# Maxima of an attention item in two parts with a turn each, one pair of maxima in every half-step

## The chip, the cores and the metric

The kernel runs on one core of one Trainium2 chip. The metric is the device time of one execution in microseconds (us), the median of several runs; lower is better. Engines are named as in the profile: PE (TensorE matmuls), PEld (its weight loads), DVE (VectorE), ACT (ScalarE), POOL (GpSimd), SP (SyncE, which issues most DMAs).

## The reference, cut to what matters

```python
x = layernorm(x + attention(x)); x = layernorm(x + ffn(x))    # x is (2, 2048, 256)

# attention: 16 heads of width 16, causal, two score matrices per head
std_logits = einsum('bhqd,bhkd->bhqk', q, k) * dh ** -0.5
geo_logits = einsum('bqhi,bkhi->bhqk', read_lines, J_write) * inc_scale  # i runs over 6
std_out = softmax(mask(std_logits)) @ v
geo_out = softmax(mask(geo_logits)) @ geo_v
combined = (1 - gate) * std_out + gate * geo_out          # gate: mean of 16 sigmoids per token
return combined @ out_w + out_b
```

## The kernel before, in words

Three stages follow one another: `project` (projections of all tokens to DRAM), `attend` (the two softmaxes) and `finish` (gate, output projection, feed-forward, the two norms). The change is in `attend`.

**Items.** `attend` works through 16 items; item `it` is one batch with two heads (a = 0, 1). A softmax over 2048 keys needs, for each query, the negated maximum of its DOT scores, so that the exponential stays in range. (The GEO maxima are only computed where `is_wide` is set; with these inputs that branch is not taken.) The maxima reach the scores as extra operand rows ("m rows") of the query operands: a score matmul adds them to the products, and ACT only takes the exponential.

**Steps and half-steps.** An item has 20 steps (`STEPS`), which cover the lower triangle in four query tiles of 512 queries (qt 0 to 3), two key blocks of 128 keys at a time; a step has one or two groups, and the change speaks of a group as a half-step. There are NPV = 36 half-steps, numbered 0 to 35 here: qt 0 is 0 to 2, qt 1 is 3 to 9, qt 2 is 10 to 20, qt 3 is 21 to 35. 28 of them are 512 queries wide and 8 are 384. In a half-step PE issues the GEO scores (L915, two matmuls side by side), the DOT scores (L921, four), and then the products with the values of a half-step of the step before (`earlier`, `times_v`, L988, f32, eight instructions). `ex` has two buffers: the scores of unit n wait until the exponential of unit n - 2 is done (L906). ACT takes one exponential per kind and half-step (L1074). POOL sets masked corners to zero (L887). DVE copies `pv` out at the end of each query tile (`take`, L1150).

**Maxima.** For the *next* item, PE computes the DOT scores once more with queries on the partitions (`max_pair`, L943): 40 pairs (`MAXT`: a query block of 128 against up to 512 keys; 28 pairs are 512 keys wide, and four each 384, 256 and 128), each pair two tiles, one per head. A tile goes into one of MX_RING = 3 PSUM banks, and DVE reduces it to a column of `mp` (L1101, or L1097 with the causal mask on the diagonal). The tile that comes three later waits for that (`mx_free`, L941). `spread` and `shares` deal the 40 pairs out over steps 0 to 16: in a step with two groups, one share goes between GEO and DOT of the first group, one between GEO and DOT of the second, and one behind DOT of the second. In step 17 (`MT_STEP`) comes `max_rows`: DVE reduces `mp` to `negm` (L1131), PE transposes it (L968), DVE splits it in two bf16 parts in `mrow` (L1139, L1141), and SP copies these to the m rows of the next item by 8 small DMAs (`rows`, L785).

**The order of SP in an item** (`item`, from L788) is written out by hand: store of the last query tile of the item before; the first six operand loads for item `it + 2` (a DMA of 128 KB each for the DOT operands); `store(it, 0)`; six more loads; in item 0 a wait for `gts_ready` and the store of the gates (L806); in item 8 the loads of the denominators of the first batch (L230, L234); `store(it, 1)`; six loads; the value operand; `store(it, 2)`; six loads; and at last `rows(it + 1)`, which waits for `mrow_ready`. PE waits for the m rows at the start of an item (`m_in`). Items 14 and 15 have no operand loads to issue.

**Prologue.** Before item 0, PE and DVE do the 40 pairs and the transposition of item 0 with nothing beside them, then DVE works out the gates (`gates_`, L1186 to L1193). The transposition of the gates is in item 0 behind step 18 (L1032), DVE copies it to `gts` (L1173), and this sets `gts_ready`, for which SP waits at L806.

**The loop.** PE's code is item 0, then a loop of four rounds of three items each (1 to 12), then items 13 to 15 written out.

Of the kernel before, what the change touches and what calls it, by code (L numbers as in the profile page):

```python
# [115 lines left out]
NMX = NTILE + 1  # L116
MX_RING = 3
MT_STEP = NSTEP - 3
# [3 lines left out]
def spread():  # L122

    room = [sum(width(s, j) for j in range(len(STEPS[s][1]))) + P if s < MT_STEP else 0 for s in range(NSTEP)]
    cost = [w + (220 if d else 150) for _, _, w, d in MAXT]
    out, u, done = [], 0, 0
    for i in range(NSTEP):
        mine = []
        while u < NMT and done + cost[u] / 2 <= sum(cost) * sum(room[:i + 1]) / sum(room):
            mine.append(u)  # L130
            done += cost[u]
            u += 1
        out.append(mine)
    assert u == NMT
    return out


MAX_IN = spread()


def shares(s):

    n, places = len(MAX_IN[s]), 1 + len(STEPS[s][1])
    out, at = [], 0
    for i in range(places):
        m = (n + places - 1 - i) // places
        out.append(MAX_IN[s][at:at + m])
        at += m
    return out
# [557 lines left out]
def attend(nc, parts, values, raw, gates, ident, mask_qk, gate_z, wide, out_w, out_b, wg, wu, wd, weights,  # L707
           sets, fixed, rden, x, late):
    with ExitStack() as ctx:
# [12 lines left out]
        mp = [sb(f"mp{i}", [P, 2 * NKB, NQT]) for i in range(2)]  # L722
        dull = sb("dull", [P, MX_RING, CH])
        negm = sb("negm", [P, P])
        mrow = sb("mrow", [4 * NKB, 2, P], BF16)
# [7 lines left out]
        m_in = sem("m_in")  # L733
# [8 lines left out]
        wx_ready = sem("wx_ready")  # L742
        wx_free = sem("wx_free")
        wx_rows = sem("wx_rows")
        negm_ready = sem("negm_ready")
        mrow_high = sem("mrow_high")
        mrow_ready = sem("mrow_ready")
# [15 lines left out]
        def _(q):  # L763
# [11 lines left out]
            def rows(it, to):  # L775

                q.wait_ge(mrow_ready, it + 1)
                q.sem_inc(passed, 1)
                for a in range(2):
                    for i in range(2):  # L780
                        geo = to["geo"][0][HALF * a + GEO_ROWS + i:HALF * a + GEO_ROWS + i + 1, :]
                        dot = to["dot"][0][HALF * a + DOT_MINOR + i:HALF * a + DOT_MINOR + i + 1, 1, :]
                        for kind, dst in ((GEO, geo), (DOT, dot)):
                            n = (2 * kind + a) * NKB
                            q.dma_start(dst.rearrange("p (k t) -> p k t", t=P),  # L785
                                        mrow[n:n + NKB, i, :]).then_inc(m_in, 16)

            def item(it):  # L788
# [40 lines left out]
                if it + 1 < ITEMS:  # L829
                    rows(it + 1, sets[(it + 1) % NSET])  # L830
# [3 lines left out]
            rows(0, sets[0])  # L834
# [9 lines left out]
        def _(g):  # L844

            g.memset(negm[:, :], 0.0).then_inc(cleared, 1)
            for i in range(2):
                g.wait_ge(cleared, i + 1)
                g.memset(mp[i][:, :, :], MASKED).then_inc(cleared, 1)
            g.wait_ge(cleared, 3)  # L850
# [48 lines left out]
        def _(pe):  # L899
# [26 lines left out]
            def max_pair(nxt, u):  # L926

                nit, which, use = nxt
                q_set, k_set = sets[which]["dot"]
                first = isinstance(nit, int) and nit == 0  # L930
                if u == 0:

                    pe.wait_ge(sets[which]["dot_in"], (use + 1) * LOADS * 16)
                    if not first:
                        pe.wait_ge(mrow_ready, nit)
                qb, k0, w, _ = MAXT[u]
                for a in range(2):
                    t = 2 * u + a
                    if t >= MX_RING:

                        pe.wait_ge(mx_free, nit * NTILE + t + 1 - MX_RING)  # L941
                    rows = slice(HALF * a, HALF * a + DOT_MAIN)
                    pe.matmul(mx[:, t % MX_RING, 0:w], q_set[rows, 0, qb * P:(qb + 1) * P],  # L943
                              k_set[rows, 0, k0:k0 + w], start=True, stop=True).then_inc(mx_ready, 1)

            def wide_pair(nxt, u):
                nit, which, use = nxt
                q_set, k_set = sets[which]["geo"]
                if u == 0:
                    pe.wait_ge(mx_free, nit * NTILE + NTILE)  # L950
                    pe.wait_ge(sets[which]["geo_in"], (use + 1) * LOADS * 16)
                else:

                    pe.wait_ge(wx_free, nit * NMT + u)
# [5 lines left out]
                last.then_inc(wx_ready, 1)  # L960

            def max_rows(nxt):
                with pe.If(is_wide > 0):
                    for u in range(NMT):
                        wide_pair(nxt, u)

                pe.wait_ge(negm_ready, nxt[0] + 1)
                pe.transpose(mx[:, (NMX - 1) % MX_RING, 0:P], negm[:, :], ident[:, :]).then_inc(mx_ready, 1)  # L968

            def times_v(it, which, use, s, j, head):  # L970
# [10 lines left out]
                if s == FIRST_OF[qt] and j == 0 and not (head and qt == 0):  # L981

                    pe.wait_ge(on_ready, it * NQT + qt)
# [11 lines left out]
            def step(at, before, nxt, s, head):  # L995

                it, which, use = at
                places = shares(s) if nxt else [[] for _ in range(1 + len(STEPS[s][1]))]
                groups = len(STEPS[s][1])

                def some(i):
                    for u in places[i]:
                        max_pair(nxt, u)
# [18 lines left out]
            def item(at, before, nxt, head):  # L1022
# [11 lines left out]
                if head:  # L1034

                    pe.wait_ge(gts_ready, 1)
# [4 lines left out]
            def prologue():  # L1041
                for u in range(NMT):
                    max_pair(static(0), u)
                max_rows(static(0))
# [39 lines left out]
        def _(v):  # L1084
            v.wait_ge(cleared, 3)
            is_wide = v.value_load(wide[0:1, 0:1], min_val=0, max_val=1)

            def max_pair(nit, u):
                qb, k0, w, on_diagonal = MAXT[u]
                for a in range(2):  # L1090
                    t = 2 * u + a
                    to = mp[DOT][:, a * NKB + qb, k0 // CH:k0 // CH + 1]

                    v.wait_ge(mx_ready, nit * NMX + t + 1)
                    if on_diagonal:
                        v.sem_inc(v_passed, 1)
                        last = v.tensor_tensor_reduce(  # L1097
                            out=dull[:, t % MX_RING, 0:w], in0=mx[:, t % MX_RING, 0:w], in1=mask_qk[:, CH - w:CH],
                            scale=1.0, scalar=3 * MASKED, op0=ALU.add, op1=ALU.max, accum_out=to)
                    else:  # L1100
                        last = v.tensor_reduce(out=to, in_=mx[:, t % MX_RING, 0:w], axis=AX.X, op=ALU.max)  # L1101
                    last.then_inc(mx_free, 1)
# [475 lines left out]
```

## Time and profile before

| | |
|---|---|
| median of 3 runs | 1913.83 us (1912.52 to 1914.31) |
| the profiled execution's own time | 1911.92 us |
| its span, first to last instruction | 1910.2 us |
| mean granted TensorE clock | 0.944 |
| PE busy | 1686.7 us (88%) |
| ACT busy | 1218.8 us (64%) |
| DVE busy | 1057.9 us (55%) |
| POOL busy | 336.5 us (18%) |
| idle of ACT before an exponential, ended by PE's GEO scores | 256.0 us |

The stage `project` runs to about 229 us of the span, `attend` to about 1568 us, `finish` to the end. A profile's groups give, for each line, engine and form, the busy time, the mean duration and the idle time of the engine just ahead of it with what ended it. The timeline gives the start and the length of runs of equal instructions in order; the length of a run of matmuls reaches from its first start to its last (modelled) end.

### The profile page before, as it was taken

Reading aid. Unit: us, or ns where it says so; the run is one execution under the profiler, and the core shown is the slowest. Engines: PE = TensorE matmul, PEld = TensorE weight load, DVE = VectorE, ACT = ScalarE, POOL = GpSimd, SP = SyncE. Lnnn points to the kernel's source line nnn. Section 1 sums busy time; section 2 is a strip of 40 time slices with the busy share of each in tenths; the row PEclk is TensorE's granted clock in tenths of the full one; section 3 lists DMA queues with packets and bytes.
Section 4 is the critical chain, followed back from the end, with each engine's and each line's share of the span. In section 5 each row is a group of like instructions: output and inputs, shape, how many; then the busy total and the mean of one; then the engine's idle time right before and its main releaser. Section 6 shows DMA issues by size and latency. Waiting matters only on the chain. (4 is left out here: it accounts for less than half of the span.)

```text
span 1910.2 us, 36280 instructions
## 1 busy us (share of the span) xinstructions
PE 1686.7 (88%) x11793; PEld 606.2 (32%) x11793; DVE 1057.9 (55%) x2509; ACT 1218.8 (64%) x1457; POOL 336.5 (18%) x478
## 2 busy tenths in 40 slices
PE   7887469679999999999989999999999874999998
PEld 4544112122222222222222222222222222565555
DVE  4775586355755657556565565755756103545432
ACT  3553308568888788887878878888888861211221
POOL 4432402012111111111111111111110213112000
PEclk9998659889999999999999999999999987999999
DMA  5774511112211111111120111111102004232000
GB/s 170 215 216 145 164 62 41 63 45 77 87 44 67 44 61 73 42 61 57 51 86 34 67 45 59 73 42 62 71 33 68 18 25 152 72 101 97 11 22 22
DMA packets 97400, 140.67 MB, mean 74 GB/s; under 512 B 8144, under 2 KB 66320, under 8 KB 95152
## 3 DMA queue, kind: packets, MB, share of 16 engines
q1 hardware_dynamic: 96000, 135.08, 20.6%
q0 software_dynamic: 624, 2.75, 0.4%
q8 instruction: 111, 1.82, 0.4%
q14 instruction: 89, 0.73, 0.1%
q10 hardware_dynamic: 576, 0.28, 0.1%
HBM read 81.96 MB, written 55.61 MB: 72 GB/s over the span
## 5 line engine op out<-in xcount | busy, mean ns | idle before, releaser
L1074 ACT ACTIVATE prob<-ex 128x1024 f32<-128x1024 f32 (+1 forms) x1152 | 1050.2, 978 | 276.9 <-PE ex L915 256.0
L1101 DVE TENSOR_REDUCE mp<-mx 128x1 f32<-128x512 f32 x768 | 487.9, 685 | 170.2 <-PE mx L943 170.2
L988 PE MATMUL pv<-prob,va 128*32 128x512 f32 (+3 forms) x5120 | 581.1, 545 | 0.6 <-POOL prob L887 0.6
L887 POOL TENSOR_SCALAR_AFFINE_SELECT prob<-prob 128x256 f32<-128x256 f32 (+1 forms) x384 | 186.1, 485 | 1124.1 <-ACT prob L1074 1119.9
L1097 DVE CUSTOM_DVE_ANT_0 dull<-mx,mask_qk 128x128 f32<-128x128 f32 (+3 forms) x512 | 231.5, 487 | 258.1 <-PE mx L943 256.5
L921 PE MATMUL ex<-dq,dk 34*128 34x512 bf16 (+7 forms) x2560 | 344.5, 352 | 29.3 <-ACT prob L1074 28.6
L943 PE MATMUL mx<-dk,dq 64*128 64x512 bf16 (+3 forms) x1280 | 305.0, 363 | 40.4 <-DVE mp L1101 20.5
L915 PE MATMUL ex<-gq,gk 38*128 38x512 bf16 (+3 forms) x1280 | 221.4, 358 | 46.0 <-DMA dq<-mrow 34.4
L915 PEld LDWEIGHTS ex<-gq,gk 38*128 38x128 bf16 x1280 | 57.3, 93 | 440.4 <-ACT prob L1074 368.5
L988 PEld LDWEIGHTS pv<-prob,va 128*32 128x32 f32 x5120 | 115.2, 109 | 227.9 <-issue 191.4
L1427 ACT ACTIVATE sg<-pg 128x512 f32<-128x512 f32 x48 | 28.7, 597 | 246.0 <-PE pg L1367 243.1
L921 PEld LDWEIGHTS ex<-dq,dk 64*128 64x128 bf16 (+1 forms) x2560 | 99.4, 95 | 175.3 <-ACT prob L1074 131.2
L943 PEld LDWEIGHTS mx<-dk,dq 64*128 64x128 bf16 x1280 | 86.8, 96 | 159.2 <-DVE mp L1101 90.5
L1150 DVE COPY on<-pv 128x512 f32<-128x512 f32 x64 | 44.3, 692 | 99.6 <-PE pv L988 98.8
L470 POOL TENSOR_TENSOR sp<-d,sp 128x512 bf16<-128x512 f32 (+1 forms) x48 | 68.8, 1448 | 141.0 <-ACT sp L565 141.0
L1367 PE MATMUL pg<-y_t,wg_f 128*128 128x512 f32 x192 | 90.8, 595 | 1.8 <-DVE ht L1507 1.7
L1367 PE MATMUL pg<-y_t,wu_f 128*128 128x512 f32 x192 | 90.2, 592 | 0.0
L1383 PE MATMUL po<-wd_f,ht 128*128 128x256 f32 x384 | 85.0, 381 | 5.7 <-DVE ht L1507 5.7
L489 PE MATMUL pn<-wv,xc 128*128 128x512 f32 x128 | 64.4, 628 | 22.5 <-DVE vn L641 14.4
L1383 PEld LDWEIGHTS po<-wd_f,ht 128*128 128x128 f32 x384 | 72.3, 190 | 17.6 <-issue 5.1
L508 PE MATMUL pr<-xc,wqk 128*128 128x512 f32 x128 | 63.8, 656 | 14.9 <-ACT sp L559 14.9
L1507 DVE SCALAR_TENSOR_TENSOR ht<-pg,sg 128x512 f32<-128x512 f32 x48 | 33.0, 690 | 76.7 <-ACT sg L1427 76.7
(98 smaller groups left out, 886.8 us busy)
## 6 DMA issues: line engine op xcount, KB each, us to landing
values<-vn SPq DMA_DIRECT2D x32, 512.0 KB, 5.2
va<-values SPq DMA_DIRECT2D x16, 1024.0 KB, 13.3
raw<-on SPq DMA_DIRECT2D x64, 256.0 KB
parts_dot<-sp SPq DMA_DIRECT2D x32, 384.0 KB, 5.0
dq<-parts_dot SPq DMA_DIRECT2D x96, 128.0 KB
dk<-parts_dot SPq DMA_DIRECT2D x96, 128.0 KB
att<-raw SPq DMA_DIRECT2D x32, 256.0 KB
rr<-rden SPq DMA_DIRECT2D x32, 256.0 KB
```

The lines of the kernel that those rows point to most:

```text
L470: g.tensor_tensor(out=sp3[m][0:n, SLOTS[m][2], :], in0=d32[m][0:n, :], in1=sp3[m][0:n, SLOTS[m][1], :], op=ALU.subtract).then_inc(p3_done, 1)
L489: pe.matmul(bank[:, 0, :], xc[par][:, k, tok], wv[:, k, :], start=k == 0, stop=k == NK - 1)
L887: g.affine_select(out=cut, in_=cut, compare_op=ALU.is_ge, fill=0.0, base=0, pattern=[[0, nb], [1, P]], channel_multiplier=-1).then_inc(mas ...
L915: last = pe.matmul(ex[:, n % 2, a * CH + at:a * CH + at + w], k_set[rows, keys], q_set[rows, queries], start=True, stop=True)
L921: last = pe.matmul(ex[:, n % 2, a * CH + at:a * CH + at + w], k_set[rows, part, keys], q_set[rows, part, queries], start=part == 0, stop=p ...
L943: pe.matmul(mx[:, t % MX_RING, 0:w], q_set[rows, 0, qb * P:(qb + 1) * P], k_set[rows, 0, k0:k0 + w], start=True, stop=True).then_inc(mx_re ...
L988: last = pe.matmul(pv[blk * VW:(blk + 1) * VW, CH - w:CH], sets[which]["v"][:, kb, blk * VW:(blk + 1) * VW], prob[UNIT_AT[s, j, kind] % NP ...
L1074: act.activation(prob[n % NPROB][:, :].rearrange("p (b c) -> p b c", b=2)[:, :, 0:w], ex[:, n % 2, :].rearrange("p (b c) -> p b c", b=2)[: ...
L1097: last = v.tensor_tensor_reduce(out=dull[:, t % MX_RING, 0:w], in0=mx[:, t % MX_RING, 0:w], in1=mask_qk[:, CH - w:CH], scale=1.0, scalar=3 ...
L1101: last = v.tensor_reduce(out=to, in_=mx[:, t % MX_RING, 0:w], axis=AX.X, op=ALU.max)
L1367: last = pe.matmul(pg[m % 2][:, i, :], w[:, k, m * P:(m + 1) * P], y_t[:, k, :], start=k == 0, stop=k == NK - 1)
L1383: last = pe.matmul(po[tt % 2][:, 0:D], ht[:, m, tt * P:(tt + 1) * P], wdf[:, m, :], start=m == 0, stop=m == NM - 1)
```

## The change

The 40 pairs of an item are split in two parts: EARLY holds the 24 pairs of query tiles 0 to 2, LATE the 16 pairs of query tile 3. Each part has its own `negm`, `mrow`, semaphores and turn. The EARLY turn stands in half-step 30 of the item before. The LATE turn stands in half-step 9 of the item itself. Pairs stand only between the GEO and the DOT scores of a half-step. `max_places` gives these places (an entry is the keys of the pair, all in one half-step):

| half-step | pairs |
|---|---|
| 0 to 8 | LATE of this item, one pair of 512 each |
| 9 | none; LATE turn |
| 10 | EARLY of the next item: 128, 256 and 384 |
| 11 to 27 | EARLY: one pair each (512; 384 in half-steps 19 and 20) |
| 28, 29 | EARLY: 128 and 256 in each |
| 30 | none; EARLY turn |
| 31 | LATE of the next item: 128, 256 and 384 |
| 32 to 35 | LATE: one pair of 512 each |

The prologue is what stands in half-steps 10 to 35, without scores; the first 9 LATE pairs of every item are now in the item. SP's `rows` is called twice per item: for LATE behind the second six operand loads, ahead of `store(it, 1)`, with 4 rows of 128 values per DMA; for EARLY at the end as before, with 12 rows per DMA (before: 16). PE waits for the EARLY m rows at the start of an item and for the LATE ones ahead of step 12 (half-step 21). The transposition of the gates and their copy to `gts` move from item 0 to the prologue, behind the EARLY turn, and use `pv` for it.

```diff
-MAX_IN = spread()
+PARTS = ((0, 1, 2), (3,))
+EARLY, LATE = 0, 1
+TURN = (30, 9)
...
+    early = [cuts(0, 0, 1, 2), cuts(0, 3)] + fulls(1) + [cuts(1, 3)] + fulls(2)[0:2] + [cuts(1, 2), cuts(2, 2)]
+    early += fulls(2)[2:] + [cuts(2, 3), cuts(1, 0, 1), cuts(2, 0, 1)]
+    late = [cuts(3, 0, 1, 2)] + fulls(3) + [cuts(3, 3)]
...
+MAX_IN = max_places()
+LEAD = TURN[LATE] + 1
...
-            def rows(it, to):
-
-                q.wait_ge(mrow_ready, it + 1)
+            def rows(it, part, to):
+
+                q.wait_ge(mrow_ready[part], it + 1)
                 q.sem_inc(passed, 1)
+                n, first = PART_BLOCKS[part], PART_FIRST[part] * P
+                cols = slice(first, first + n * P)
...
                             q.dma_start(dst.rearrange("p (k t) -> p k t", t=P),
-                                        mrow[n:n + NKB, i, :]).then_inc(m_in, 16)
+                                        mrow[part][at:at + n, i, :]).then_inc(m_in[part], 16)
...
                     load_den(q, raw, gates, 0, late)
+                rows(it, LATE, sets[it % NSET])
                 store(it, 1)
                 load(range(12, 18))
...
-                    rows(it + 1, sets[(it + 1) % NSET])
+                    rows(it + 1, EARLY, sets[(it + 1) % NSET])
...
                 for j in range(groups):
+                    h = PV_AT[s, j]
+                    to = at if h < LEAD else nxt
                     scores(it, which, s, j, GEO, head)
-                    some(j)
+                    if to:
+                        for u in MAX_IN[h]:
+                            max_pair(it, to, u)
                     scores(it, which, s, j, DOT, head)
-                    if j == groups - 1:
-                        some(groups)
-                    if j == 0 and s == MT_STEP and nxt:
-                        max_rows(nxt)
+                    if to and h in TURN:
+                        turn(it, to, TURN.index(h))
                     earlier(j)
...
-                pe.wait_ge(m_in, (it + 1) * 128)
+                pe.wait_ge(m_in[EARLY], (it + 1) * 128)
                 for s in range(NSTEP):
+                    if s == FIRST_OF[PARTS[LATE][0]]:
+                        pe.wait_ge(m_in[LATE], (it + 1) * 128)
                     step(at, before, nxt, s, head)
-                    if head and s == NSTEP - 2:
-
-                        pe.wait_ge(gate_ready, 5)
-                        pe.transpose(mx[0:2 * NC * TT, 0, 0:P], gate[:, :, :].rearrange("p i n -> p (i n)"),
-                                     ident[:, :]).then_inc(gate_turned, 1)
...
             def prologue():
-                for u in range(NMT):
-                    max_pair(static(0), u)
-                max_rows(static(0))
+                for h in range(LEAD, NPV):
+                    for u in MAX_IN[h]:
+                        max_pair(-1, static(0), u)
+                    if h in TURN:
+                        turn(-1, static(0), TURN.index(h))
+
+                        pe.wait_ge(gate_ready, 5)
+                        pe.transpose(pv[0:2 * NC * TT, 0:P], gate[:, :, :].rearrange("p i n -> p (i n)"),
+                                     ident[:, :]).then_inc(gate_turned, 1)
```

## Rows read from the trace of the kernel before

**Rows 1.** Waits of PE, whole span: us in total, times, longest
```profile
PE ex L915 <- DMA dq<-mrow: 34.4, 2, 27.4
```
**Rows 2.** Timeline of PE, item 12, half-steps 16 and 17 (start, length)
```profile
1290.27 0.39 PE L915 MATMUL ex<-gq,gk 38*128 38x512 bf16 x2
1292.24 0.39 PE L915 MATMUL ex<-gq,gk 38*128 38x512 bf16 x2
...
1293.22 0.80 PE L943 MATMUL mx<-dk,dq 64*128 64x512 bf16 x2
...
1294.95 0.39 PE L915 MATMUL ex<-gq,gk 38*128 38x512 bf16 x2
```
**Rows 3.** Timeline of the prologue: DVE's first tile, PE's sixth
```profile
232.18 0.29 DVE L1097 CUSTOM_DVE_ANT_0 dull<-mx,mask_qk 128x128 f32<-128x128 f32 x1 [8.49 <-PE mx L943]
...
233.16 0.10 PEld L943 LDWEIGHTS mx<-dk,dq 64*128 64x128 bf16 x1 [0.27 <-DVE mp L1097]
```
**Rows 4.** Timeline of PE: the transposition of item 12
```profile
1323.68 0.33 PE L968 MATMUL mx<-ident,negm 128*128 128x128 f32 x1
```
**Rows 5.** Timeline of PE: GEO scores of half-steps 0 and 21, and next item
```profile
1256.65 0.39 PE L915 MATMUL ex<-gq,gk 38*128 38x512 bf16 x2
...
1301.35 0.39 PE L915 MATMUL ex<-gq,gk 38*128 38x512 bf16 x2
...
1333.09 0.39 PE L915 MATMUL ex<-gq,gk 38*128 38x512 bf16 x2
```
**Rows 6.** Timeline of SP, item 12: first store, last of twelve loads issued
```profile
1259.28 0.55 SPq L772 DMA_DIRECT2D raw<-on  x1
...
1281.67 4.78 SPq L225 DMA_DIRECT2D dk<-parts_dot  x3
```
**Rows 7.** The page's DMA issues: count, KB each
```profile
raw<-on SPq DMA_DIRECT2D x64, 256.0 KB
...
dq<-parts_dot SPq DMA_DIRECT2D x96, 128.0 KB
```
**Rows 8.** Windows: busy us per engine, PEclk, DMA share of 16 engines, GB/s
```profile
1260.00:1301.00 41.00, 39.49 (x356) 11.12 (x352) 29.60 (x72) 34.76 (x39) 7.26 (x15) 1.00 0.13 52
```
**Rows 9.** Timeline: the m rows of item 1 and the gate they wait behind
```profile
361.97 0.53 SPq L806 DMA_DIRECT2D gates<-gts  x1
...
383.35 0.59 SPq L785 DMA_DIRECT2D dq<-mrow  x1
...
391.24 0.61 PE L915 MATMUL ex<-gq,gk 38*128 38x512 bf16 x2 [27.37 <-DMA dq<-mrow]
```
**Rows 10.** Line L785, all m row DMAs: issue to landing
```profile
DMA to landing us min/median/max: 1.7/1.8/7.8
```
**Rows 11.** Timeline, item 8: denominators' gates issued by SP, awaited by DVE
```profile
969.38 2.51 SPq L234 DMA_DIRECT2D den_gate<-gates  x2
...
984.89 3.35 DVE L241 RECIPROCAL den<-den 128x512 f32<-128x512 f32 x1 [5.46 <-DMA den_gate<-gates]
```
**Rows 12.** Timeline of PE: transposition of the prologue, first scores of item 0
```profile
278.18 0.47 PE L968 MATMUL mx<-ident,negm 128*128 128x128 f32 x1 [3.60 <-DVE negm L1131]
...
285.73 0.61 PE L915 MATMUL ex<-gq,gk 38*128 38x512 bf16 x2 [7.07 <-DMA dq<-mrow]
```
**Rows 13.** Windows before and after the last operand load of the prologue
```profile
274.00:278.00 4.00, 0.59 (x1) 0.08 (x1) 1.90 (x6) 0.00 (x0) 0.00 (x0) 0.50 0.13 51
278.00:280.00 2.00, 0.47 (x1) 0.18 (x1) 1.36 (x5) 0.00 (x0) 0.00 (x0) 0.50 0.01 4
```
**Rows 14.** Timeline of PE: start of item 7
```profile
857.32 0.61 PE L915 MATMUL ex<-gq,gk 38*128 38x512 bf16 x2 [2.53 <-issue]
```
**Rows 15.** Windows: the same place, PEclk and the rest
```profile
857.00:868.00 11.00, 10.61 (x72) 3.82 (x72) 4.50 (x18) 5.49 (x7) 2.91 (x6) 0.53 0.08 23
```
**Rows 16.** Timeline of DVE, item 15
```profile
1494.26 2.28 DVE L1178 TENSOR_TENSOR att<-att,rr 128x2048 f32<-128x2048 f32 x1
```
**Rows 17.** Groups of DVE by form: a full tile of maxima, count, busy, mean ns
```profile
L1101 DVE TENSOR_REDUCE mp<-mx 128x1 f32<-128x512 f32 x768 | 487.9, 685 | 170.2 <-PE mx L943 170.2
```

More of the change, by code:

```diff
@@ L115 @@
 NTILE = 2 * NMT
-NMX = NTILE + 1
 MX_RING = 3
-MT_STEP = NSTEP - 3
 DEN_STEP = 10
[L122 to L134, printed above, removed]
-    return out
@@ L138 @@
-MAX_IN = spread()
[L141 to L149, printed above, removed]
+PARTS = ((0, 1, 2), (3,))
+EARLY, LATE = 0, 1
+TURN = (30, 9)
+PART_BLOCKS = [TT * len(qts) for qts in PARTS]
+PART_FIRST = [TT * qts[0] for qts in PARTS]
+PART_OF = [next(p for p in range(2) if qb // TT in PARTS[p]) for qb, _, _, _ in MAXT]
@@ new lines, with __init__, add, ready @@
+MAX_IN = max_places()
+LEAD = TURN[LATE] + 1
+class Ring:
+    def __init__(self):
+        self.order, self.bank, self.tiles, self.part = [], [], [], []
+        at, tiles = 0, 0
+        for h in range(NPV):
+            for u in MAX_IN[h]:
+                for a in range(2):
+                    self.add((u, a), at % MX_RING, tiles, None)
+                    at, tiles = at + 1, tiles + 1
+            for part in range(2):
+                if h == TURN[part]:
+                    self.add(("turn", part), at % MX_RING, None, part)
+                    at += 1 if part == EARLY else 3
+            if h == LEAD - 1:
+                self.head, self.head_tiles = len(self.order), tiles
+        assert tiles == NTILE and at % MX_RING == 0
+        self.uses = len(self.order)
+        self.place = {use: i for i, use in enumerate(self.order)}
+    def add(self, use, bank, tile, part):
+        self.order.append(use)
+        self.bank.append(bank)
+        self.tiles.append(tile)
+        self.part.append(part)
+    def ready(self, it, i):
+        return (it + 1) * self.uses - self.head + i + 1
+    def freed(self, it, i):
+        return (it + 1) * NTILE - self.head_tiles + self.tiles[i] + 1
+    def owner(self, i):
+        j = i - 1
+        while self.bank[j] != self.bank[i]:
+            j -= 1
+        return j % self.uses, j < 0
@@ L152, in set_of, with item_of @@
+RING = Ring()
+EARLY_FIRST = MAX_IN[LEAD][0]
+def item_of(it, part):
+    return it + 1 if part == EARLY else it
 def set_of(k, i):
@@ L731, in attend @@
         pv = pb("pv", [P, CH])
-        m_in = sem("m_in")
+        m_in = [sem(f"m_in{p}") for p in range(2)]
         cleared = sem("cleared")
@@ L980, in times_v @@
                     pe.wait_ge(sets[which]["v_in"], (use + 1) * 16)
-                if s == FIRST_OF[qt] and j == 0 and not (head and qt == 0):
-                    pe.wait_ge(on_ready, it * NQT + qt)
+                if s == FIRST_OF[qt] and j == 0:
+                    if head and qt == 0:
+                        pe.wait_ge(gts_ready, 1)
+                    else:
+                        pe.wait_ge(on_ready, it * NQT + qt)
                 at = 0
@@ L1089, in max_pair @@
+            def max_pair(it, u):
                 qb, k0, w, on_diagonal = MAXT[u]
                 for a in range(2):
-                    t = 2 * u + a
-                    to = mp[DOT][:, a * NKB + qb, k0 // CH:k0 // CH + 1]
-                    v.wait_ge(mx_ready, nit * NMX + t + 1)
+                    i = RING.place[u, a]
+                    v.wait_ge(mx_ready, RING.ready(it, i))
                     if on_diagonal:
                         v.sem_inc(v_passed, 1)
[L1097 to L1101, printed above, removed]
```

205 lines of the change are left out of this document (113 added, 92 removed).

## The prediction

> **What bounds the kernel now.** I read the waits of PE first, then the timelines. The largest wait of PE in `attend` is for m rows, 34.4 us in two waits [rows 1]: one before item 0, one of 27.4 us before item 1. Inside an item I compared half-steps. With one pair between GEO and DOT, the next GEO comes 1.97 us later (1290.27 to 1292.24); with a second pair behind DOT it is 2.71 us (1292.24 to 1294.95), because its tiles, 0.80 us long instead of 0.39, wait for a bank that DVE has not emptied [rows 2]. The last item, without maxima, isn't faster per half-step than with one pair: one pair hides in the wait of DOT for the exponential. So the double pairs are what a stream of one pair can save. An item in the steady middle lasts 76.44 us (1256.65 to 1333.09), of which 44.70 lie before half-step 21 (1301.35) and 31.74 behind it [rows 5].
>
> A third resource nearly fills the item: SP's DMAs. From 1260 to 1301 their share is a flat 0.13, some two of 16 engines, at 52 GB/s [rows 8]. SP has issued the last of the twelve loads by 1286.5 [rows 6], but what stands in the queue, two stores of 256 KB and twelve loads of 128 KB [rows 7], is 2.1 MB and takes 40.3 us at 52 GB/s: from 1260 to about 1300.5. The queue is 14 us behind SP.
>
> **The change, part by part.** All terms are in us of the profiled execution (1911.92).
>
> *Gates in the prologue.* Before, SP stands at the wait for `gts_ready` until 361.97, and everything behind it in SP's order is late; the last m row of item 1 is issued at 383.35 and PE starts item 1 at 391.24, after 27.37 us idle [rows 9]. With the gates ready before item 0, SP runs ahead as in other items: -27.4.
>
> *A shorter prologue.* The 9 LATE pairs of half-steps 0 to 8 leave it: 18 full tiles at 0.635 (487.9 / 768) [rows 17], 11.4. The EARLY m rows can now fly while DVE does the gates and the other LATE tiles, which ended with PE's start at 285.73 at the latest [rows 12], so at 274.3 now. But the two busy DMA engines still carry the loads of item 1: share 0.13 until 278, 0.01 after that [rows 13]. The m rows stand behind these, and land in 1.8 (median) [rows 10]: start at 279.6, so -6.1. Bounds: -11.4 and 0.
>
> *LATE m rows in the item.* They are issued behind the twelve loads, at 1286.5 on item 12's scale, and PE needs them at half-step 21. If they stood alone they would land about 7 us later (eight issues of 0.6, then 1.8), at 1293.5, in time. I hold that they don't stand alone. An m row DMA behind a full queue landed 7.8 after its issue instead of 1.8 [rows 10], and it was item 1's, PE waiting [rows 9]. In item 8 another DMA, issued just behind the same twelve loads, from 969.38, landed at 984.89, some 13 us after its issue had ended (969.38 + 2.51) [rows 11]. So the LATE m rows land when the queue has drained, 1300.5 to 1301, plus 1.8 and a little for eight small DMAs: 1303.2. PE would be ready at 1301.35 or, with what half-steps 0 to 20 save, at 1300.2: their double pairs go (0.7 each for those of two full pairs, as in rows 2, less for the short ones, 2.5 in all), six tiles in half-step 10 (1.1, priced below) and the second transposition, 0.33 [rows 4], come. So PE waits 3 us and resumes 46.5 into the item instead of 44.7: +1.8 per item. What is saved before half-step 21 is lost in this wait. Bounds: -1.1 (landed in time) and +3.
>
> The Trainium skill, "DMA: Bandwidth & Descriptors", section "Why a DMA increments its semaphore by 16 and not by 1", says that such a DMA is spread over as many engines, at most 16, as divide the slowest dimension of both sides, and takes the lowest-numbered ones. By this rule the loads (slowest dimension 2) sit on two engines, as the share of 0.13 shows, and LATE's 4 rows on four engines that include these two; no run here shows which engines a DMA of 4 rows takes. By the rule the sum stands; if it did not hold, the sum would be that of the first rival.
>
> *Half-steps 21 to 35.* Gone: the double pairs of half-steps 22, 24 and 28, scaled from the 0.74 of [rows 2] by their width: about 0.25 + 0.5 + 0.7 = 1.45. New: half-steps 28 and 29 have two cut pairs ahead of DOT, 31 has three. The prologue shows the price of six such tiles in three banks: the sixth starts 0.98 after DVE began the first [rows 3]. A tile's matmul starts 0.2 behind GEO, DVE begins 0.4 to 0.5 later, so DOT starts 1.6 behind GEO instead of 0.5: +1.1. With four tiles it is about 1.1 instead of 0.5: +0.6, twice. The LATE pairs in 32 to 35 hide as others do: +0.1 (0 to +1). The EARLY turn costs what it cost before. Together -1.45 + 1.1 + 1.2 + 0.1 = +1.0 (bounds -1 and +2.5).
>
> *Sum per item:* +2.8. It holds in items 1 to 7 and 9 to 13 (12 items). Four of them (1, 4, 7, 10) begin with a disturbed stretch that the wait now covers, so I count 1.8 there: 8 x 2.8 + 4 x 1.8 = +29.6. In item 8 PE already waits near half-step 21 for DVE and the denominators: +1. Item 14 has no loads, so no wait: -1.1 + 1.0, about 0. Item 15 now has LATE pairs, and DVE's 2.28 for `att` [rows 16] and 1.2 for the mix stand in the middle of them: +2.5. In item 0 the queue has a head start: 0.
>
> *TensorE's clock.* Before item 7 PE was idle for 2.53, and then 0.53 of full speed was granted on average over the next 11 us, that is the 1.2 GHz level for most of it [rows 14, 15]. A wait of 3 us at half-step 21 should do the same at times. In such a stretch ACT bounds two of three half-steps, so it costs less than the half: between 0 and 3, I take 1.4 in 12 items: +17.
>
> SP issues 8 more DMAs per item (5 us); before, it stood waiting about 10 us for the turn, so this is free, and the second turn costs DVE under 1 us of idle time. EARLY m rows leave one half-step sooner: no cost.
>
> **Sum:** -27.4 - 6.1 + 29.6 + 1 + 2.5 + 17 = +16.6, so 1928.5 for the profiled execution. The median of the runs shown lies 1.9 above that execution (1913.83 against 1911.92): **1930.4**.
>
> **The rivals.**
> 1. *LATE m rows land in time*, being small and on engines that are free. For it: at a share of 0.13 some 14 of 16 engines are free [rows 8], and 1.8 is the median landing [rows 10]. Against: the two rows of late landings above. Then each item is -1.1 + 1.0, about 0, nothing is idle and the clock holds: -27.4 - 6.1 + 2.5 = -31, **1883** with the 1.9. The point: landing before 44 us of the item. Chance 0.18.
> 2. *The wait is there, but the clock holds* or the wait is nearer 2 us: the 17 fall away, **1913**, within the noise of the measurement, which can't tell less than about 0.2% (4 us) from no change. Chance 0.18.
> 3. *The stream is better than I price it*: six tiles cost little since PE can place them beside DOT in other rows of the array, -1 instead of +1 behind half-step 21 takes 24 from the twelve items, and the clock drops in half of them, 8 less: 1930.4 - 32 = **1898**. Chance 0.12.
> 4. *The change doesn't do what it says*: the stream isn't even (three half-steps hold two or three pairs). That is in my sum.
>
> My forecast with its neighbours, slower, has 0.52. Slower by over 0.2%: 0.52 and a third of rival 2, 0.58. Within 0.2%: 0.13. Faster: the rest, 0.29. The forecast's own range is 1919 to 1946. The whole range is 1888 to 1947: it reaches down to rival 3 and leaves out rival 1 at 1883 and the highest costs of clock and wait, some 0.2 together.
>
> **What would show it.** PE's waits: a new one at L915 for the DMA of `mrow` of 2 to 4 us in some 12 items, and the one of 27 us gone; item 0 starting near 280; GEO of half-step 21 at 46.5 of the item, the item 79 to 81 long; waits of L943 for DVE in half-steps 10, 28, 29 and 31; a lower mean clock in `attend`. The landing of L785's DMAs would have two groups. Wrong is the forecast if PE does not wait at half-step 21.

## The result: slower, and by more than forecast

| | before | after |
|---|---|---|
| median | 1913.17 us, shared runs (1911.44 to 1914.31) | 1953.66 us of 4 runs (1952.89 to 1961.90) |
| ratio | 1 | 1.0222, 95% interval 1.0194 to 1.0251 |
| profiled execution | 1911.92 us | 1961.90 us |
| mean granted TensorE clock | 0.944 | 0.934 |

The forecast was 1930.4 (1888 to 1947). Its direction was right, its size too small by 23 us, and the time lies outside its range. The profiled execution of after is the slowest of its four, 8 us above their median. I compare profile with profile below (+50.0 us) and median with median in the experiments; so some 8 of the 50 us are this execution's own. One of the 11 executions of before beside e1 to e4 took 3938 us, and the ratios leave it out.

The page of after, busy times and one of its groups (line engine op, tiles, count, busy, mean ns, idle before):

```profile
PE 1693.0 (86%) x11809; PEld 601.8 (31%) x11809; DVE 1083.8 (55%) x2557; ACT 1230.1 (63%) x1457; POOL 337.4 (17%) x479
...
L1164 DVE TENSOR_REDUCE mp<-mx 128x1 f32<-128x512 f32 x768 | 492.3, 686 | 321.4 <-PE mx L1008 302.2
```

A full tile of maxima takes DVE 686 ns, as before [rows 17]. PE's busy time grew by 6.3 us of the 50, DVE's by 26, but DVE is busy for only 55% of the span. So PE's time went into idle stretches. Waits of PE in after (us in total, times, longest):

```profile
PE ex L973 <- DMA dq<-mrow: 40.3, 14, 9.0
...
PE mx L1008 <- DVE mp L1161: 35.3, 73, 1.7
```

The one wait of 27.4 for the gates is gone from [rows 1]. What is left are a wait before item 0 (9.0, before 7.1) and, new, one at half-step 21 of 13 items. Waits of DVE in after, those that no other engine ends ("issue"); the same view of before lists none at these two lines, only 2.1 us once at `negm` and 0.3 at a masked tile:

```profile
DVE mp L1164 <- issue: 16.2, 4, 4.1
DVE on L1221 <- issue: 4.7, 4, 1.3
```

This is the row that I had not reckoned with. Item 12, the item of [rows 2], [rows 5] and [rows 6], shows both. Timeline of PE in after: GEO of half-steps 0, 21, 28 to 32, and of the next item:

```profile
1282.96 0.39 PE L973 MATMUL ex<-gq,gk 38*128 38x512 bf16 x2
...
1333.02 0.39 PE L973 MATMUL ex<-gq,gk 38*128 38x512 bf16 x2 [3.39 <-DMA dq<-mrow]
...
1349.09 0.39 PE L973 MATMUL ex<-gq,gk 38*128 38x512 bf16 x2
...
1351.72 0.39 PE L973 MATMUL ex<-gq,gk 38*128 38x512 bf16 x2
...
1354.35 0.39 PE L973 MATMUL ex<-gq,gk 38*128 38x512 bf16 x2
...
1356.37 0.39 PE L973 MATMUL ex<-gq,gk 38*128 38x512 bf16 x2
...
1359.81 0.39 PE L973 MATMUL ex<-gq,gk 38*128 38x512 bf16 x2
...
1368.17 0.39 PE L973 MATMUL ex<-gq,gk 38*128 38x512 bf16 x2
```

The item lasts 85.21 instead of 76.44: 50.06 before half-step 21 (before: 44.70), and 35.15 behind it (31.74). Half-steps 28 and 29, with two cut pairs ahead of DOT, take 2.63 each, 31 with three takes 3.44.

DVE in after at the start of the same item, and then SP:

```profile
1281.08 1.29 DVE L1164 TENSOR_REDUCE mp<-mx 128x1 f32<-128x512 f32 x2 [0.57 <-PE mx L1008]
1286.41 1.29 DVE L1164 TENSOR_REDUCE mp<-mx 128x1 f32<-128x512 f32 x2 [4.04 <-issue]
1287.62 0.68 DVE L1221 COPY on<-pv 128x512 f32<-128x512 f32 x1
```
```profile
1288.39 0.55 SPq L827 DMA_DIRECT2D raw<-on  x1
...
1296.04 14.71 SPq L280 DMA_DIRECT2D dq<-parts_dot  x3
1310.79 4.78 SPq L280 DMA_DIRECT2D dk<-parts_dot  x3
1315.69 2.23 SPq L842 DMA_DIRECT2D gq<-mrow  x1
...
1322.14 0.57 SPq L842 DMA_DIRECT2D dq<-mrow  x1
```

DVE stands idle for 4.04 us between the last pair of one item and the first of the next, though PE's first tile of the new item, started at 1283.18, is done by 1283.6. This is where DVE's own loop (one item per round) jumps back: in the trace of after the branch stands on DVE's sequencer (which issues its instructions) at 1281.28, the first instruction of the next round (it sets registers) at 1284.07, and the one after it at 1286.41. Before, the same place lay in steps 17 to 19, which had no pairs. The branch stands at 1248.11, the next instruction at 1250.86, and DVE is idle there for 8.98 us anyway, with PE as the releaser. DVE in before:

```profile
1257.29 0.29 DVE L1097 CUSTOM_DVE_ANT_0 dull<-mx,mask_qk 128x128 f32<-128x128 f32 x1 [8.98 <-PE mx L943]
...
1258.50 0.69 DVE L1150 COPY on<-pv 128x512 f32<-128x512 f32 x1 [0.60 <-PE pv L988]
```

In after pairs stand on both sides of the jump. PE's pair must wait for a bank, DVE's copy of `pv` comes 4.7 into the item instead of 1.85, SP's first store, which waits for that copy, 5.4 instead of 2.6 [rows 6], and all of SP's order with it: the last LATE m row is issued 39.2 into the item and PE's wait for it ends at 50.06.

**Where the 50.0 us went.** Each half-step is measured from the start of its first exponential to the next; sums are after less before, in the profiled executions, beside what the prediction's terms say.

```
                                    predicted   measured
start of item 0                        -6.1        -5.9
length of item 0 (the gates)          -27.4       -26.5
items 1 to 14, half-steps 0 to 20     +17.5       +51.9
    of it half-steps 0 to 2                       +16.5
    half-steps 3 to 19                             +3.0
    half-step 20 (ends in the wait)               +32.5
items 1 to 14, half-steps 21 to 35    +30.0       +27.2
item 15                                +2.5        +3.5
sum                                   +16.5       +50.2
```

(The prediction's 17.5: 8 items of +1.8, 4 of +0.8, item 8 +1, item 14 -1.1. Its 30.0: 13 items of +1.0 and 17 for the clock.) One line is wrong, by 34.4. The others are off by up to 2.8 each, and their misses nearly cancel (0.7 together).

### The profile page after: what moved, and what is told of

Its sections match the earlier page's. It is cut to its first block and busy times, and to the rows that moved or that the text cites. A ratio compares the mean times of both kernels' runs of the same rounds, so it can differ in the third digit from the quotient of the medians.

```text
span 1960.2 us, 36600 instructions
## 1 busy us (share of the span) xinstructions
PE 1693.0 (86%) x11809; PEld 601.8 (31%) x11809; DVE 1083.8 (55%) x2557; ACT 1230.1 (63%) x1457; POOL 337.4 (17%) x479
## 3 DMA queue, kind: packets, MB, share of 16 engines
q8 instruction: 111, 1.82, 0.4%
## 5 line engine op out<-in xcount | busy, mean ns | idle before, releaser
L1145 ACT ACTIVATE prob<-ex 128x1024 f32<-128x1024 f32 (+1 forms) x1152 | 1061.5, 977 | 315.8 <-PE ex L973 234.1
L1062 PE MATMUL pv<-prob,va 128*32 128x512 f32 (+3 forms) x5120 | 594.0, 556 | 0.5 <-POOL prob L945 0.5
L979 PE MATMUL ex<-dq,dk 34*128 34x512 bf16 (+7 forms) x2560 | 356.1, 360 | 23.2 <-ACT prob L1145 19.9
L1008 PE MATMUL mx<-dk,dq 64*128 64x512 bf16 (+3 forms) x1280 | 276.0, 370 | 68.8 <-DVE mp L1161 35.3
L973 PE MATMUL ex<-gq,gk 38*128 38x512 bf16 (+3 forms) x1280 | 227.3, 367 | 65.3 <-DMA dq<-mrow 40.3
L979 PEld LDWEIGHTS ex<-dq,dk 34*128 34x128 bf16 (+1 forms) x2560 | 102.1, 97 | 182.3 <-ACT prob L1145 148.2
L1008 PEld LDWEIGHTS mx<-dk,dq 64*128 64x128 bf16 x1280 | 81.7, 96 | 134.5 <-DVE mp L1161 73.8
```

Source lines behind the costliest of these rows:

```text
L973: last = pe.matmul(ex[:, n % 2, a * CH + at:a * CH + at + w], k_set[rows, keys], q_set[rows, queries], start=True, stop=True)
L979: last = pe.matmul(ex[:, n % 2, a * CH + at:a * CH + at + w], k_set[rows, part, keys], q_set[rows, part, queries], start=part == 0, stop=p ...
L1008: pe.matmul(mx[:, RING.bank[i], 0:w], q_set[rows, 0, qb * P:(qb + 1) * P], k_set[rows, 0, k0:k0 + w], start=True, stop=True).then_inc(mx_r ...
L1062: last = pe.matmul(pv[blk * VW:(blk + 1) * VW, CH - w:CH], sets[which]["v"][:, kb, blk * VW:(blk + 1) * VW], prob[UNIT_AT[s, j, kind] % NP ...
L1145: act.activation(prob[n % NPROB][:, :].rearrange("p (b c) -> p b c", b=2)[:, :, 0:w], ex[:, n % 2, :].rearrange("p (b c) -> p b c", b=2)[: ...
```

## Experiments

**Theories.** A, the prediction's: the LATE m rows are late because their DMAs queue behind operand loads that move at 52 GB/s on few DMA engines. B: DVE's jump costs PE some 2.5 us per item by itself and delays SP's order, which adds to A's wait. C, the rival to both: the stream itself, with its bunches of pairs in half-steps 10, 28, 29 and 31, is the loss, and the waits would only move.

**e1, e2, e3: the two waits alone and together.** e1 writes DVE's items out, so that it has no loop:

```diff
-            with v.Fori(1, PAIRS_OF_HEADS) as it:
-                item(it, False, True)
-            item(PAIRS_OF_HEADS, False, True)
-            with v.Fori(PAIRS_OF_HEADS + 1, ITEMS - 1) as it:
-                item(it, False, True)
+            for it in range(1, ITEMS - 1):
+                item(it, False, True)
```

> The changed kernel with DVE's two loops over items 1 to 7 and 9 to 14 written out, nothing else. Theory A (DVE's jump back at the end of a loop round costs it about 3 to 4 us; before, it fell in steps 17 to 19, where DVE had no pairs, now pairs stand on both sides of it): the idle time of about 4 us ahead of DVE's first tile of an item is gone in items 2 to 7 and 10 to 14, half-steps 1 and 2 together take 4.2 us as in items 1, 4 and 9 instead of 7 to 8.6, and the stores of SP, with the whole DMA queue, come 2 to 3 us earlier. Part of it is taken back by a longer wait for the LATE m rows at half-step 21, so 1953.7 falls to 1932 to 1948. Rival B (DVE is late for another reason, for instance the copy of pv or the m rows): nothing moves, 1950 to 1957.

e2 issues the LATE m rows ahead of the second six loads:

```diff
                 store(it, 0)
+                rows(it, LATE, sets[it % NSET])
                 load(range(6, 12))
...
-                rows(it, LATE, sets[it % NSET])
                 store(it, 1)
```

> The changed kernel with the 8 DMAs of the LATE m rows issued ahead of the second six operand loads instead of behind them. Theory A (they land late because they stand in the rings behind twelve loads that two DMA engines work off): PE's wait for them at half-step 21 (now 2 to 4 us in 12 items) is gone, half-steps 0 to 20 take 46 to 47 us instead of 48 to 50, the clock drops less often, 1953.7 falls by 30 to 45, to 1909 to 1924. Rival B (small DMAs of 4 rows are slow by themselves, or mrow is ready late): the wait stays, 1945 to 1957.

e3 does both.

> Both edits: DVE's items written out and the LATE m rows first. Theory A for both: an item takes 43.6 + 33.1 = 76.7 us, nothing waits for m rows or for DVE's jump: 1883 to 1895, clearly under the sum of what each edit brings alone, since alone the one's gain is partly taken by the other's wait. Rival: the two gains add up or the queue finds another wait: over 1900.

Measured against the kernel before (1912.94 in these runs): e1 1940.23 (ratio 1.0147, 1.0117 to 1.0176), e2 1921.20 (1.0043, 1.0021 to 1.0065), e3 1883.28 (0.9851, 0.9821 to 0.9881). All three lie in the ranges expected. Taken from 1953.66, e1 gives back 13.4, e2 32.5, both 70.4. The two costs hide each other: with only DVE's jump gone PE is at half-step 21 earlier and waits longer there; with only the wait gone the jump's loss remains. Waits of PE in e1:

```profile
PE ex L973 <- DMA dq<-mrow: 56.2, 14, 9.1
```

e1 is the kernel that the prediction priced, the change without a cost of DVE's loop. Its half-steps 0 to 20 of items 1 to 14 are 31.4 longer than before, where the prediction's terms say 17.5, and its median is 9.8 above the forecast. So this line was priced 14 too low without any cost of DVE's loop, and the waits for the LATE m rows are why: in the twelve items besides item 8 PE waits 3.1 to 4.1 us, and half-steps 0 to 20 are 2.6 to 3.0 longer in the eight steady ones instead of 1.8; in item 8 they are 5.0 longer instead of 1. The other 20.5 of the table's 34.4 come from DVE's loop.

In e3, where only the one before item 0 is left:

```profile
PE ex L973 <- DMA dq<-mrow: 8.9, 1, 8.9
```

e3's item 12 on PE, GEO of half-steps 0 and 21 and of the next item, and DVE at its start:

```profile
1222.99 0.39 PE L973 MATMUL ex<-gq,gk 38*128 38x512 bf16 x2
...
1266.81 0.39 PE L973 MATMUL ex<-gq,gk 38*128 38x512 bf16 x2
...
1299.69 0.39 PE L973 MATMUL ex<-gq,gk 38*128 38x512 bf16 x2
```
```profile
1223.63 1.29 DVE L1164 TENSOR_REDUCE mp<-mx 128x1 f32<-128x512 f32 x2 [1.23 <-PE mx L1008]
1224.89 0.69 DVE L1221 COPY on<-pv 128x512 f32<-128x512 f32 x1
```

The item is 76.70 long, 43.82 + 32.88. The idle 4 us of DVE are gone and its copy comes 1.9 into the item, as before the change. In e3 half-steps 0 to 2 of items 1 to 14 sum to 7.9 less than before and 3 to 19 to 6.9 less; in after they were 16.5 and 3.0 more. The difference is 24.4 + 9.9 = 34.3; between e2 and e3, which differ in DVE's loop alone, it is 23.4 + 9.2 = 32.6, some 2.4 us per item. That this is near the table's miss of 34.4 is chance: with the loop's loss PE comes later to half-step 21 and waits less there, so in after the loop costs 20.5, and the rest is the wait. A and B both hold. C doesn't: without the two waits the kernel is 30 us faster than before.

**e4: how much of that is the stream?** The kernel before, with nothing but the transposition and copy of the gates moved into the prologue (for PE; DVE's copy moves the same way, and PE waits for `gts_ready` before `pv` is first used):

```diff
                     step(at, before, nxt, s, head)
-                    if head and s == NSTEP - 2:
-                        pe.wait_ge(gate_ready, 5)
-                        pe.transpose(mx[...], gate[...], ident[:, :]).then_inc(gate_turned, 1)
-                if head:
-                    pe.wait_ge(gts_ready, 1)
...
                 max_rows(static(0))
+                pe.wait_ge(gate_ready, 5)
+                pe.transpose(pv[...], gate[...], ident[:, :]).then_inc(gate_turned, 1)
```

> The kernel before with one part of the change alone: the gates are transposed and copied in the prologue. Theory: PE's wait of 27.4 us ahead of item 1 is gone and nothing else changes: 1913.2 falls to 1883 to 1887. Rival (SP is late in item 0 for its queue as well, and the wait only shrinks): 1890 to 1905.

Measured: 1880.08 (0.9844, 0.9814 to 0.9874), 32.9 below its 1912.94 and 3 below the range expected. Item 1 starts at

```profile
363.33 0.39 PE L915 MATMUL ex<-gq,gk 38*128 38x512 bf16 x2
```

on PE, instead of after the wait that ended at 391.24 [rows 9]; its steady items keep their 76.43. So e3, with the even stream, is no faster than e4 without it (1883.3 and 1880.1): the gates are the whole gain of e3, and the even stream brought 0.9 per item in half-steps 0 to 20 and lost 1.15 behind them.

**e5: the bunches.** In e3 a half-step with several pairs keeps one between GEO and DOT and puts the others behind DOT:

```diff
-                        for u in MAX_IN[h]:
+                        for u in MAX_IN[h][:1]:
                             max_pair(it, to, u)
                     scores(it, which, s, j, DOT, head)
+                    if to:
+                        for u in MAX_IN[h][1:]:
+                            max_pair(it, to, u)
```

> The kernel of e3 (DVE's items written out, LATE m rows first), and in half-steps with more than one pair only the first pair stands between GEO and DOT, the others behind DOT. Theory (the even stream's gain is eaten by half-steps 10, 28, 29 and 31, where DOT stands behind 4 or 6 tiles in 3 banks: 3.08, 2.63, 2.63 and 3.29 us in e3): they fall to about 2.3, 2.2, 2.2 and 2.6, an item of 76.7 to 74.4, 1883.3 to 1850 to 1860. Rival (DVE's time for the six tiles decides, wherever they stand): 1875 to 1886.

Measured: 1863.36, against 1908.78 of before in these runs (0.9755, 0.9739 to 0.9771), 3 above what was expected. GEO of half-steps 28 to 32 on PE:

```profile
1266.67 0.39 PE L973 MATMUL ex<-gq,gk 38*128 38x512 bf16 x2
...
1268.87 0.39 PE L973 MATMUL ex<-gq,gk 38*128 38x512 bf16 x2
...
1271.07 0.39 PE L973 MATMUL ex<-gq,gk 38*128 38x512 bf16 x2
...
1273.17 0.39 PE L973 MATMUL ex<-gq,gk 38*128 38x512 bf16 x2
...
1276.23 0.39 PE L973 MATMUL ex<-gq,gk 38*128 38x512 bf16 x2
```

28 and 29 fell from 2.63 to 2.20, as expected. 31 fell only from 3.29 to 3.06, where 2.6 was expected, and 10 from 3.08 to 2.72 instead of 2.3: three pairs are too much for a half-step wherever they stand. The item is 75.33, so the stream is now worth 1.1 per item over before's 76.43.

**e6 and e7: the queue itself.** Each operand load, whose slowest dimension is 2, becomes two DMAs whose slowest dimension is the rows (16 or 6), half the size each:

```diff
...
-        rows = dst[row:row + 2 * n, :] if kind == GEO else dst[row:row + 2 * n, int(minor), :]
-        q.dma_start(rows, src).then_inc(to[("geo_in", "dot_in")[kind]], 16)
+        for half in range(2):
+            at = row + half * n
+            rows = dst[at:at + n, :] if kind == GEO else dst[at:at + n, int(minor), :]
+            q.dma_start(rows, src[half]).then_inc(to[("geo_in", "dot_in")[kind]], 16)
...
```

(Left out are the two halves of `src` and PE's waits, which now count twice the loads.)

e6 is after with this edit alone, e7 is e5 with it.

> The changed kernel, its order of SP kept, with each operand DMA of 2 x n rows issued as two DMAs of n rows (16 or 6 rows as slowest dimension instead of 2; the same bytes). Theory (the twelve loads keep two DMA engines busy for 30 us, and the LATE m rows wait behind them): the share of DMA engines while loads run rises well over 0.13 and they are done at once, the m rows land within 2 us of their issue, and PE's wait at half-step 21 is gone as in e2: 1905 to 1925. Rival (the loads are slow for their size or their DRAM rows, not for the number of engines): the share stays at 0.13, 1945 to 1960.

> e5 with the operand loads split as in e6, for the fastest version. Theory: the queue held nothing up in e5 except in item 8, where DVE waits for the denominators that stand behind twelve loads and PE loses about 9 us: 4 to 9 us less than e5. Rival: nothing waits for the queue any more, 0 to 1 us; or SP's 24 more issues of 0.6 us make the EARLY m rows late, 5 to 20 us more.

Measured: e6 1885.02 (0.9883, 0.9864 to 0.9902), e7 1826.40 (0.9563, 0.9545 to 0.9582). Both are faster than was expected, by 20 us or more. e6 in 41 us of its item 12 (columns as in [rows 8]), and its second twelve issues on SP:

```profile
1212.00:1253.00 41.00, 37.35 (x320) 10.02 (x324) 26.56 (x59) 32.78 (x36) 5.41 (x11) 0.96 0.29 92
```
```profile
1221.39 2.79 SPq L282 DMA_DIRECT2D dq<-parts_dot  x6
1224.22 3.57 SPq L282 DMA_DIRECT2D dk<-parts_dot  x6
```

Over as long a stretch as [rows 8] the share is 0.29 instead of 0.13 and the rate 92 GB/s instead of 52. SP issues these six loads, now twelve DMAs, in 6.4 us, where after needs 19.5 for six (14.71 and 4.78, from 1296.04 on), and e6 has no wait for m rows left. This is theory A shown directly: the order of the issues is that of after, and only the shape of the loads differs. The Trainium skill, "DMA: Bandwidth & Descriptors", section "Why a DMA increments its semaphore by 16 and not by 1", has a DMA spread over the largest number up to 16 that divides the slowest dimensions of both sides. The trace agrees: 2 gives a flat 0.13, 16 and 6 rows more than double it.

What was not expected lies ahead of item 0. PE in e5: the first tile of the prologue, and the first scores of item 0:

```profile
231.82 0.47 PE L1008 MATMUL mx<-dk,dq 64*128 64x128 bf16 x3 [12.39 <-issue]
...
280.22 0.61 PE L973 MATMUL ex<-gq,gk 38*128 38x512 bf16 x2 [8.94 <-DMA dq<-mrow]
```

and in e7:

```profile
212.74 0.48 PE L1010 MATMUL mx<-dk,dq 64*128 64x128 bf16 x3 [12.49 <-issue]
...
251.70 0.93 PE L975 MATMUL ex<-gq,gk 38*128 38x512 bf16 x2
```

The prologue starts 19.1 earlier, because in `project` stores and operand loads share SP's order, and the wait of 8.94 for the m rows is gone: 28 together. Item 8 falls from 88.45 to 79.17, another 9.3, since the denominators' DMA no longer queues.

**e8, e9: what of this is the load split, and does DVE's jump still count?** e8 is e4 with the split loads; e9 is e7 with DVE's loop back.

> The kernel before (whole turn, doubled pairs) with the gates in the prologue and the operand loads each in two DMAs. Theory: the 28 us that the split brought ahead of item 0 in e6 and e7 come from the stage project and the prologue, whose DMAs no longer stand behind the loads, and have nothing to do with the two parts. Then item 0 of this kernel starts some 28 earlier than in e4, items 1 to 7 and 9 to 14 stay at 76.4, item 8 loses some 5: 1880 - 28 - 5 = 1847 (1840 to 1853), 21 above e7. Rival: the gain ahead of item 0 needs the shorter prologue of the two parts (fewer m rows ahead of item 0); then 1862 or more.

> e7 with one thing undone: DVE's loop of one item per round is back. Theory: the jump of DVE costs about 4 us of its time in half-steps 0 to 2 and delays PE by itself, whatever SP and the m rows do: as e2 against e3 (38 us over 14 items, 2.7 each), so 1826 + 38 = 1864 (1855 to 1870), items of 78, half-steps 21 to 35 at 31.9 as in e7. Rival: the jump only hurts through SP's queue (late store, late m rows); with the split loads that queue has air, and the time is 1826 to 1835.

Measured: e8 1856.71 (0.9709, 0.9672 to 0.9746), e9 1860.22 (0.9730, 0.9701 to 0.9760), before 1912.44. e8 missed its range by 4. Its item 0 starts on PE at

```profile
264.69 0.61 PE L917 MATMUL ex<-gq,gk 38*128 38x512 bf16 x2 [1.25 <-DMA dq<-mrow]
```

19.5 ahead of e4's, not 28. The theory was right for those 19 and the rival for the rest: e7, with the shorter prologue, starts 13.0 before e8, but after only 4.4 before e4 (279.83 and 284.20). The nine pairs taken out of the prologue are worth 4.4 while the m rows queue behind the loads and 13.0 when they don't.

e9 lies in its range, 33.8 above e7. Waits of DVE in e9:

```profile
DVE mp L1169 <- issue: 16.5, 4, 4.2
...
DVE on L1226 <- issue: 4.6, 4, 1.2
```

e7 has neither. SP's queue has air in both, so the jump costs PE directly: half-steps 0 to 19 of items 1 to 14 are 34.7 longer in e9 than in e7, again 2.5 per item on average.

Writing the loop out takes away more than the jump, and the items tell the parts apart. Items 2 to 7 and 10 to 14 come after a jump: 2, 3, 5 and 6 lose 3.2 to 3.5 each, 11 to 14 lose 4.1 to 5.4; items 4, 7 and 10, where PE's own loop jumps at the same time, -0.9, 0.4 and 1.7. Items 1 and 9 run in the loop's code too, but no jump stands ahead of them: they lose 0.43 each, all of it in half-step 10. Item 8, outside the loops, loses nothing. So the jump is 29 of the 34.7, and nearly all of the rest, 5.4, is the loop's code in half-step 10.

e7 is the best version here: 1826.4, 4.4% below before. e8 needs only two small edits of the kernel before and has 2.9% of it; the two-part maxima (with e5's placing, the order of e2 and DVE written out) add 30 us: 13 at the start and 21 in items 1 to 14 (1.1 in a steady item, 3 to 4 in items 4, 7 and 10), while item 15 gives 2 back. The before of e8 and e9 is 3.7 above that of e7; by the ratios these are 28 us, and e9 is 32 above e7.

## Why the prediction was wrong, and where it was right

- **The first step that failed:** "the second turn costs DVE under 1 us of idle time". I priced what the turn costs DVE and nothing else of DVE's program. The LATE pairs that the change puts in half-steps 32 to 35 and 0 to 8 stand on both sides of DVE's jump back, and I counted them at "The LATE pairs in 32 to 35 hide as others do: +0.1" and at nothing. What was missing is the cover: DVE was idle for 8.98 us at that place before, and the jump was in it. Measured: 13.4 us of the medians with the waits for m rows in place (after less e1), 37.9 without them (e2 less e3); 20.5 of the table's 34.4.
- **The second: the LATE m rows** came late for the reason given, but later than "resumes 46.5 into the item". The last of them was awaited in 13 items. Where DVE's jump did no harm (items 1 and 9) PE waited 3.7 and 3.1 us and half-step 20 ended at 48.3 and 47.5 of the item; in e1 most items have 47.3. Without wait and jump (e3) PE is there at 43.8; I said 43.5. So the landing was put 1 to 2 us too early, and the term for half-steps 0 to 20, 17.5, measures 31.4 in e1. That is why e1 misses the forecast by 9.8 us (other terms give some of it back); e1 still lies in the forecast's range, and after, with the jump, doesn't.
- **Half-steps 21 to 35:** +1.15 per item in e3, +1.0 predicted. The bunches were the cost, as e5 shows: 28 and 29 together gave back 0.86. In after they were 2.63 long as reckoned (1.97 and 2.07 plus 0.6). Half-steps 10 and 31 were 3.08 and 3.29 in e3 and 1.82 and 2.23 before: +1.26 and +1.06, priced at +1.1. In after they were 3.60 and 3.44, so DVE's loop lengthens these bunches too, also in items 1 and 9 without a jump ahead. In the traces each tile of maxima in the loop's code has one more instruction ahead of its wait on DVE's sequencer (ALU_OP, 0.04 us; 88 in item 12 of after, none in e3), and DVE's short tiles leave little time for it; that this is the reason is argued, not shown.
- **The clock:** the mean fell from 0.944 to 0.934, and behind a wait the granted clock did fall. Windows of after around item 12's half-step 21 (columns as in [rows 8]):

```profile
1321.00:1333.00 12.00, 8.63 (x82) 2.13 (x78) 4.94 (x14) 7.53 (x9) 2.91 (x6) 1.00 0.18 60
1333.00:1345.00 12.00, 11.82 (x80) 2.84 (x80) 7.14 (x11) 9.33 (x10) 0.00 (x0) 0.72 0.31 121
```

  From full speed it goes to 0.72 on average, so a part of the second window ran at 1.2 GHz; PE had been idle for 3.39 us just before. Seven items of the twelve had it (1, 4, 6, 7, 9, 10 and 12, with waits of 2.5 to 3.7 us); the other five, with waits of 0.3 to 1.8 us, kept full speed. Against e3 the seven lost 1.0 to 2.3 us from half-step 21 on, item 6 4.2 (1.4 in half-step 21 itself in items 1, 4 and 10), 14.4 together. I had 1.4 in twelve items, 17. The line of the table is +27.2 and e3's 17.0, only 10 apart, because item 8 is 5.0 shorter there than in e3. In e1, where all twelve items wait, ten had a lower clock, and the twelve lost 14.7 against e3; items 9 and 12 waited 3.4 us and kept full speed. No run separates the clock from everything else, but the size was near.
- **The gates:** -27.4 predicted, -26.5 in the profiles, -32.9 in the medians of e4. In e4's profile item 0 is 26.6 shorter; the rest lies in the start of item 0 (1.6) and in half-steps 0 to 2 of later items (5.1), mostly of items 1, 7 and 10, and no run says why.
- **The prologue:** -6.1 predicted, -5.9 measured. The reason, m rows behind the loads, is the 9.00 us that PE waits before item 0, and e7 against e8 shows the bound of -11.4 coming true, and a little more (-13.0), when that queue is gone.
- **Item 15:** +2.5 predicted, +3.5 measured.
- **Rivals.** Rival 1 (m rows in time, 1883) is what e3 made true: 1883.28. It was a good price for a case that did not happen, with some luck in the last digits: in e3 the gates, the start and half-steps 0 to 20 are within 0.6 of its terms, and half-steps 21 to 35 are 3 longer. Rivals 2 and 3 did not happen. None of my cases had an engine's own control flow in it, and the upper end of the range was set from the waits alone.

## What to carry to other kernels

When work is moved in time on an engine, look at what that engine does at the places it is moved to, its loop's jump included: idle time with another releaser can hide a cost of the engine's own that shows only once work stands on both sides of it. Two waits in a row on one path hide each other, so undo them singly and together before either is called small (13.4 and 32.5 alone, 70.4 together). Judge the size of one cause in a run without the others: in after the waits look as large as forecast, in e1 they are larger. And a flat DMA share of 2 in 16 beside small urgent DMAs is a shape to mend early: here the split of the loads brought 23 to 69 us in each of three versions.

## What the runs showed of the hardware that was not expected

- **DVE's jump back leaves it idle for up to 4.2 us.** The second of DVE's two loops shows it before items 11 to 14 (16.2 us in 4 waits in after, of which e3 has 1.23 each anyway, waiting for PE); in the first, the rows show 1.1 to 1.3 ahead of the copy in items 2, 3, 5 and 6. The two differ by where a second pause falls. At each of the 11 jumps 2.7 to 3.0 us pass from the branch to the next instruction. In the second loop another 2.3 us follow at once (1284.07 to 1286.41); in the first, DVE does the two tiles of a pair in between (443.26 to 445.63 in item 2). The Trainium skill, "Runtime: NRT & Kernel Launch", section "Instruction fetch mechanics", says that a taken branch to instructions outside the two blocks at hand makes the sequencer fetch them first. The trace agrees. A queue of instructions, q14, moves three packets from 1281 to 1288 us of after, at 1282.3, 1284.7 and 1287.1, the time of this jump. It has one in as long a stretch at the start of items 1 and 9, where DVE enters a loop without a jump, and none from 1217 to 1227 in e3, around the start of item 12. These are its packets and MB from 1281 to 1288 in after, in all of after, and in all of e3:

```profile
q14 instruction: 3, 0.02, 1.2%
...
q14 instruction: 101, 0.83, 0.1%
...
q14 instruction: 60, 0.49, 0.1%
```

  So instructions are fetched while DVE pauses, and only with the loop; that the whole pause is this fetch is argued and not shown. PE's own loop, at another place, shows 2.5 to 2.7 us three times per execution in before [rows 14] and 2.2 to 2.8 in after.
- **Splitting loads in two halves paid well beyond the wait that it was meant for:** 68.6 us in after (1953.66 to 1885.02), 37.0 in e5 (1863.36 to 1826.40), 23.4 in e4 (1880.08 to 1856.71). By the ratios to each run's own before these are 65, 37 and 26. SP's own issues were held up by the queue: three loads took up to 14.71 us to issue in after (item 12), the six DMAs of three split loads 2.63 to 3.57 in e6.
- Not tried: which DMA engines a DMA of 4 m rows takes; pairs moved away from DVE's jump with the loop kept; a placing without three pairs in one half-step.
